# Mixer's second product: two images in every second slot, its followers a slot later, a quarter of the activations on ScalarE

## The reference, cut to what matters

```python
xh = _dht2d(x).reshape(B, H, W, nb, bs)
xn = jnp.roll(jnp.flip(xh, axis=(1, 2)), shift=(1, 1), axis=(1, 2))
...
o1k = relu(0.5 * (xh w1a + xn w1b) + b1[0])
o1n = relu(0.5 * (xn w1a + xh w1b) + b1[1])
...
o2k = 0.5 * (o1k w2a + o1n w2b) + b2[0]
o2n = 0.5 * (o1n w2a + o2k w2b) + b2[1]
y = (o2k + o2n).reshape(B, H, W, C)
y = jnp.sign(y) * jax.nn.relu(jnp.abs(y) - SPARSITY)
y = _dht2d(y) / (W * C)
return y + bias
```

## Time and profile before

| | us |
|---|---|
| median of 3 runs | 110.15 (109.63 to 111.55) |
| the profiled execution | 110.37 |
| its span in the trace | 108.6 |
| slots 8 and 9 (start of line 792's first matmul to start of slot 10) | 23.94 to 29.05 |
| slots 10 and 11 | 29.05 to 36.42 |
| slots 12 to 15 | 36.42 to 47.68 |
| slots 16 to 19 | 47.68 to 60.10 |
| slot 20 up to its first line 732 | 60.10 to 62.45 |

### The profile page before, as it was taken

One profiled execution on the slowest core, in us unless ns is written; L12 is line 12 of the kernel. 1 busy time (PEld: TensorE's weight loads), 2 busy tenths in 40 slices (PEclk: granted clock), 3 DMA queues, 4 the chain that ended last, 5 costly groups with the idle time before them and its releaser, 6 DMA issues.

```text
span 108.6 us, 2853 instructions
## 1 busy us (share of the span) xinstructions
PE 100.9 (93%) x1008; PEld 87.7 (81%) x1008; DVE 70.3 (65%) x282; ACT 63.6 (59%) x186; POOL 55.2 (51%) x107
## 2 busy tenths in 40 slices
PE   5799999999999999999889799998899999999990
PEld 4488898988898799988669598875899999999670
DVE  1117687786877787773534879797576956665761
ACT  5036985928643776646426595867566557667520
POOL 1108500000888598885004264669998997753300
PEclk9999999999999999999999999999999999999999
DMA  2898800000000000000000000000000010011122
GB/s 73 245 348 227 329 12 6 0 3 0 3 0 6 0 0 0 6 0 0 0 6 0 0 12 0 0 0 6 0 0 0 0 48 31 26 48 51 48 68 77
DMA packets 3182, 4.57 MB, mean 42 GB/s; under 512 B 480, under 2 KB 2400, under 8 KB 3168
## 3 DMA queue, kind: packets, MB, share of 16 engines
q1 hardware_dynamic: 2160, 2.61, 7.3%
q10 hardware_dynamic: 1008, 1.78, 5.0%
HBM read 3.34 MB, written 1.05 MB: 40 GB/s over the span
## 4 chain that ended last, share of the span: by engine, by line
PE 77%; DVE 5%; POOL 4%; ACT 4%; DMA 3%; issue 3%; POOLq 1%; SPq 0%; DVEq 0%
PE banks L732 10%; PE banks L634 8%; PE banks L726 8%; PE banks L706 7%; PE banks L673 6%; PE banks L663 5%; PE banks L829 4%; PE banks L690 4%; PE banks L847 4%; DMA xt_in<-in_x_t 3%; PE banks L792 3%; PE banks L646 3%; PE banks L616 3%; PE banks L872 2%; PE banks L808 2%
## 5 line engine op out<-in xcount | busy, mean ns | idle before, releaser
L533 POOL TENSOR_SCALAR hidden<-first,ident_columns 64x260 f32<-64x260 f32 x16 | 19.7, 1230 | 18.6 <-DVE first L1241 17.7
L982 ACT ACTIVATE probs<-negated,lowest 128x256 f32<-128x256 f32 x48 | 23.9, 499 | 6.9 <-DVE negated L1139 6.8
L481 POOL TENSOR_TENSOR probs<-probs,inverse 128x256 f32<-128x256 f32 x30 | 17.9, 614 | 16.0 <-DVE inverse L1153 15.6
L990 ACT ACTIVATE probs_t<-banks 128x512 f32<-128x512 f32 x22 | 13.1, 595 | 9.9 <-PE banks L706 9.8
L732 PE MATMUL banks<-probs_t,v 128*128 128x256 f32 x56 | 15.2, 395 | 0.0
L1153 DVE RECIPROCAL inverse<-total 128x1 f32<-128x1 f32 x48 | 7.6, 160 | 10.3 <-ACT probs L982 9.8
L706 PE MATMUL banks<-ident_columns,probs 128*128 128x128 f32 x88 | 13.3, 273 | 0.0
L1139 DVE TENSOR_SCALAR_CACHE_REDUCE negated<-banks 128x256 f32<-128x256 f32 x32 | 12.1, 416 | 0.6 <-issue 0.2
L706 PEld LDWEIGHTS banks<-ident_columns,probs 128*128 128x128 f32 x88 | 10.5, 141 | 0.8 <-POOL probs L481 0.2
L732 PEld LDWEIGHTS banks<-probs_t,v 128*128 128x128 f32 x56 | 9.8, 190 | 1.2 <-issue 0.2
L1145 DVE TENSOR_SCALAR_CACHE_REDUCE negated<-banks,v 128x256 f32<-128x256 f32 x16 | 7.1, 482 | 4.7 <-PE banks L673 4.6
(11 more groups left out here) (122 smaller groups left out, 208.6 us busy)
## 6 DMA issues: line engine op xcount, KB each, us to landing
out<-stream SPq DMA_DIRECT2D x7, 128.0 KB, 2.0
rows<-in_x_rows ACTq DMA_DIRECT2D x1, 768.0 KB, 6.2
xt_in<-in_x_t SPq DMA_DIRECT2D x1, 512.0 KB, 5.3
constants<-in_constants SPq DMA_DIRECT2D x1, 450.0 KB, 5.6
layer<-in_layer ACTq DMA_DIRECT2D x1, 256.5 KB, 3.6
xt_in<-in_x_t SPq DMA_DIRECT2D x2, 128.0 KB, 3.6
xt_in<-in_x_t SPq DMA_DIRECT2D x1, 256.0 KB, 4.4
rows<-in_x_rows ACTq DMA_DIRECT2D x1, 256.0 KB, 4.7
```

What stands on the lines that cost most here:

```text
L481: pool.tensor_tensor(probs[:, half(job), tile, :], probs[:, half(job), tile, :], inverse[:, at, tile:tile + 1].to_broadcast([TILE, TOKENS] ...
L533: pool.tensor_scalar(halves(hidden[HC:C, half(job), side]), strided(first[own, half(job)], SUMS, -SUMS, SUMS), column["b1n"][own], 0.0, AL ...
L982: nc.scalar.activation(probs[:, half(job), tile, :], negated[:, half(job), tile, :], ACT.Exp, bias=lowest[:, half(job), tile:tile + 1], sc ...
L990: nc.scalar.activation(flat(probs_t[:, half(job)]), probs_t_bank, ACT.Copy).then_inc(probs_t_ready, 1)
```

## The change

Four things are done together.

- `second_product` runs for two images in a row, in the slots in which the younger of them is two slots old and odd. Images 0 and 1 have it in slot 11, 2 and 3 in slot 13, 4 and 5 in slot 15, 6 and 7 at the start of slot 17. ACT's `shrink_top` and DVE's `shrink` follow in pairs. `hidden` has four buffers in place of two.
- All that follows (`backward_channels`, `turn`, `backward_tokens`, `move_g`, `move_turned`, `add_turned`) belongs to the image four slots back in place of three, and so ends in slot 19 in place of 18. `turn` is now directly behind `backward_channels`.
- Images 5, 6 and 7 (before: 6 and 7) have their results in bank 4, so their `turn` waits for `move_g`, and `backward_channels` of images 6 and 7 waits for `add_turned` of the image before. `g` always goes through bank 4.
- Of the four parts of the relu one moves from POOL to ACT: `activate_last`, one activation with a bias, at the very end of ACT's slot. POOL keeps one part, DVE its two.

```diff
+def shares_g_bank(job):
+    return job.image >= BATCH - 3
+def mixed_pair(job):
+    return mixes(job) and job.image % PAIR == PAIR - 1
...
-        hidden = sb("hidden", [C, 2, 2, FREQ])
+        hidden = sb("hidden", [C, 4, 2, FREQ])
...
-            return banks[:, 4 if job.image >= BATCH - PAIR else 6 + half(job), :]
+            return banks[:, 4 if shares_g_bank(job) else 6 + half(job), :]
...
             def activate_other(job):
...
-                for side in range(2):
-                    own = slice(side * HC, (side + 1) * HC)
-                    pool.tensor_scalar(
-                        halves(hidden[HC:C, half(job), side]),
...
+                pool.tensor_scalar(
+                    halves(hidden[HC:C, i % 4, 0]), strided(first[0:HC, half(job)], SUMS, -SUMS,
...
             def energies_of_pair(job):
-                    pe.wait_ge(layer_done[MIXER], BATCH - PAIR)
+                    pe.wait_ge(layer_done[MIXER], BATCH - 3)
...
             def backward_channels(job):
-                if i == BATCH - 1:
+                if i > BATCH - 3:
                     pe.wait_ge(layer_done[MIXER], i)
...
             def turn(job):
-                if i >= BATCH - PAIR:
+                if shares_g_bank(job):
                     pe.wait_ge(g_ready, i + 1)
...
             # TensorE, slot(now)
+                if mixed_pair(back2) and not mixes(this):
+                    second_product(back3)
+                    second_product(back2)
...
-                if mixes(back2) and by_age(now, 4, 3):
-                    second_product(back2)
                 if by_age(now, 4, 3):
                     mix_values(by_age(now, 4, 3))
-                if mixes(back3):
-                    backward_channels(back3)
-                if mixes(back2) and not by_age(now, 4, 3):
+                if mixes(back4):
+                    backward_channels(back4)
+                    if not shares_g_bank(back4):
+                        turn(back4)
+                if mixed_pair(back2) and mixes(this):
+                    second_product(back3)
                     second_product(back2)
                 if mixes(this):
                     first_product(this)
...
-                if mixes(back3):
-                    turn(back3)
-                    backward_tokens(back3)
+                if mixes(back4):
+                    if shares_g_bank(back4):
+                        turn(back4)
+                    backward_tokens(back4)
...
+            def activate_last(job):
+                i = job.image
+                act.wait_ge(first_ready, i + 1)
+                if i >= 4:
+                    act.wait_ge(y_psum, i - 3)
+                nc.scalar.activation(
+                    halves(hidden[HC:C, i % 4, 1]), strided(first[HC:C, half(job)], SUMS, -SUMS,
+                                                            SUMS),
+                    ACT.Relu, bias=column["b1n"][HC:C]).then_inc(last_act_ready, 1)
...
             # ScalarE, slot(now)
-                if mixes(back2):
+                if mixed_pair(back2):
+                    shrink_top(back3)
                     shrink_top(back2)
                 if mixes(this):
                     move_of_sums(this)
-                if mixes(back3):
-                    move_turned(back3)
+                if mixes(back4):
+                    move_turned(back4)
+                if mixes(this):
+                    activate_last(this)
```

More of the change, by code:

```diff
@@ L528, in activate_other @@
                 pool.wait_ge(first_ready, i + 1)
[L529 to L536 removed]
+                if i >= 4:
+                    pool.wait_ge(y_psum, i - 3)
+                pool.tensor_scalar(
+                    halves(hidden[HC:C, i % 4, 0]), strided(first[0:HC, half(job)], SUMS, -SUMS,
+                                                            SUMS),
+                    column["b1n"][0:HC], 0.0, ALU.add, ALU.max).then_inc(other_act_ready, 1)
             def normalize(job):
@@ L830, in second_product @@
                             halves(o), second[:, side],
-                            strided(hidden[:, half(job), side], at, step, TILE // 2),
+                            strided(hidden[:, i % 4, side], at, step, TILE // 2),
                             start=True, stop=True)
@@ L900, in slot @@
             def slot(now):
-                this, back1, back2, back3 = (job_at(now, k) for k in range(4))
+                this, back1, back2, back3, back4 = (job_at(now, k) for k in range(5))
                 mean_pair, variance_pair = (completed_pair(job_at(now, k)) for k in (5, 6))
+                if mixed_pair(back2) and not mixes(this):
+                    second_product(back3)
+                    second_product(back2)
                 if plain_pair(back2):
@@ L1008, in move_g @@
                 act.wait_ge(g_psum, job.image + 1)
-                nc.scalar.activation(flat(g[:, half(job)]), g_bank(job),
+                nc.scalar.activation(flat(g[:, half(job)]), g_bank,
                                      ACT.Copy).then_inc(g_ready, 1)
+            def activate_last(job):
+                i = job.image
+                act.wait_ge(first_ready, i + 1)
+                if i >= 4:
+                    act.wait_ge(y_psum, i - 3)
+                nc.scalar.activation(
+                    halves(hidden[HC:C, i % 4, 1]), strided(first[HC:C, half(job)], SUMS, -SUMS,
+                                                            SUMS),
+                    ACT.Relu, bias=column["b1n"][HC:C]).then_inc(last_act_ready, 1)
             def move_turned(job):
                 act.wait_ge(back_psum, job.image + 1)
+                if job.image >= 2:
+                    act.wait_ge(layer_done[MIXER], job.image - 1)
                 nc.scalar.activation(turned[:, half(job)], result_bank(job)[:, TOKENS:2 * TOKENS],
@@ L1017, in slot @@
             def slot(now):
-                this, back1, back2, back3 = (job_at(now, k) for k in range(4))
+                this, _, back2, back3, back4 = (job_at(now, k) for k in range(5))
                 if by_age(now, 4, 3):
@@ L1228, in shrink @@
                     dve.wait_ge(mixer_ready, 6)
+                if i >= 2:
+                    dve.wait_ge(g_psum, i - 1)
                 nc.vector.scalar_tensor_tensor(
@@ L1246, in activate @@
                 dve.wait_ge(first_ready, i + 1)
-                if i >= 2:
-                    dve.wait_ge(y_psum, i - 1)
+                if i >= 4:
+                    dve.wait_ge(y_psum, i - 3)
                 for side in range(2):
                     own = slice(side * HC, (side + 1) * HC)
-                    nc.vector.tensor_scalar(hidden[0:HC, half(job), side], first[own, half(job)],
+                    nc.vector.tensor_scalar(hidden[0:HC, i % 4, side], first[own, half(job)],
                                             column["b1k"][own], 0.0, ALU.add, ALU.max).then_inc(
@@ L1296, in slot @@
                     sum_means(completed_pair(mixed))
-                if mixes(back3):
-                    add_turned(back3)
+                if mixes(back4):
+                    add_turned(back4)
                 if plain_pair(back2):
```

27 lines of the change are left out of this document (13 added, 14 removed).

## The result

The changed kernel takes 114.91 us (median of 7 runs, 114.51 to 118.74) against 109.94 (7 runs of the kernel before). The ratio is 1.044 (95% interval 1.041 to 1.048): 4.9 us slower by the ratio, 5.0 by the medians. Some executions of most kernels here take 2 to 4 us longer and are left out of the ratios; the profiled one of the changed kernel is such (118.74 us), and as it lost its time ahead of slot 8, which began at 27.40 us and not at 23.94, it is read from slot 8 on. From there to the end it takes 116.9 - 27.40 = 89.5 us against 108.6 - 23.94 = 84.7: 4.8 us more.

What follows compares the result with a forecast made beforehand. The prediction took PE to bound the kernel: new PE stops of 8.1 us, less 2.9 of stops that go and 0.8 of switches, give 4.4 us more on the profiled 110.37, so 114.8 us; range 112.3 to 116.4.

Steps and rivals of the forecast that it cites:

- PE's stops are what counts in the mixer: Slots 12 to 15: PE busy 11.26 us of 11.26, so only its stops count; taking work from POOL alone gains nothing.
- ACT's wait for `first` ahead of `probs_t`: Slots 9 to 11: `activate_last` waits for DVE's `first` and delays `probs_t`; PE stops of 1.50, 1.21 and 1.21 us.
- The ring: Slots 10 and 11: round of waits from line 726 through `first`, `activate_last` and `probs_t` to the next 726, 3.55 us.
- `z` late in slots 12 and 14: `z` stands behind `activate_last` on ACT, so line 808 waits: PE stops of 0.82 and 0.36 us.
- Three round trips over `g`, and `y` behind `g` on ACT: Slots 16 to 19: PE waits for `g`, and once for image 7's `y`: stops 0.42, 0.64, 0.69, 0.64, 0.64 us.
- The stop in slot 20 goes: The 0.68 us wait for DVE's weights ahead of line 634 in slot 20 disappears.
- The delay passes to the end undiminished: Behind line 732 the order is untouched and everything awaited moved with it, so no delay is given back.
- The switches, 0.76 us: Pairing second products leaves four changes of matmul width instead of eight, saving 4 x 0.19 us; by the drain rule 0.43.
- The sum: Whole kernel: stops that come 8.1 us, stops that go 2.9, switches 0.8, together 4.4 us more.
- (a): Rival: `first` is always ready when ACT comes, so its wait costs nothing; 110.1 us, no change; chance 0.09.
- (b): Rival: pairing hides the round trips over `g` too and, with (a), only gains stay; 106.7 us; chance 0.03.
- (d): Rival: PE's clock halves in slots 9 to 12 through idleness; about 120 us; chance 0.02.

Runs made afterwards that it cites:

- experiment 1: The changed kernel with both upper parts of the relu made by POOL again, pairs, late slot and bank 4 kept: 111.30 us, ratio 1.014.
- experiment 10: On experiment 8's kernel, slots 8 to 10: transposes ahead of the first product, ACT's `probs_t` copy ahead of `of_sums`: 110.08 us, ratio 1.0005.
- Experiment 4: The changed kernel with `backward_channels` of images 5 to 7 earlier in slots 17 to 19, other PE work between it and `turn`: 113.41 us, ratio 1.033.
- experiments 1 to 3: experiment 1, experiment 2, and the kernel before with only a relu quarter moved from POOL to the end of ACT's slot: 113.32 us, ratio 1.030.
- experiment 8: The kernel before with `backward_channels` of image 7 moved ahead of layer 2's projections in slot 18: 109.02 us, ratio 0.993.
- experiment 2: The changed kernel with ACT's relu activation moved behind the next slot's copies of `probs_t`, `z` and `g`: 110.77 us, ratio 1.009.

## Why the prediction was right

The forecast was 114.8 us with a range of 112.3 to 116.4, and 114.91 was measured. Point by point:

- **PE's stops are what counts in the mixer; work off POOL is worth nothing there.** Right: POOL lost 4.5 us of load in slots 12 to 15 and the slots got longer; and taking the quarter back (experiment 1) made the kernel faster. It is right for this order only: in experiment 10 POOL is on the path.
- **ACT's wait for `first` ahead of `probs_t`.** Right in place and mechanism. Forecast stops of 1.50, 1.21 and 1.21 us, measured 31.85 - 30.23 = 1.62 (line 799 starts at 29.78 and takes 0.45), then 1.33 and 1.33. The ring is 3.66 us and not 3.55. The term that was mis-sized is the distance from `activate_last` to `probs_t`: 0.53 us for the 0.40 taken from the exponential. It lies above the upper bound of the prediction too (0.49), because the overlap is missing that each of the prediction's rows had.
- **`z` late in slots 12 and 14.** Forecast stops 0.82 and 0.36, measured 0.89 and 0.47, in the main from the same 0.13 us.
- **Three round trips over `g`, and `y` behind `g` on ACT.** Forecast 0.42, 0.64, 0.69, 0.64, 0.64; measured 0.42, 0.63, 0.64, 0.63, 0.64. Experiment 4 removes the three ahead of line 870, and shows what the prediction didn't have: that DVE's order is the next thing behind them.
- **The stop in slot 20 goes.** Right: line 641 has no idle ahead of it at 69.81, and line 739 follows at 70.83.
- **The delay passes to the end undiminished.** Right: 46.07 us against 46.15.
- **The switches, 0.76 us.** Too small. Two images took 2 x (0.59 + 0.42) = 2.02 us for lines 829 and 808 in the chain; a slot with a pair takes 1.02 + 0.42 for the same two lines, and the slot without one 0.23. The chain of the changed kernel in slot 13:

```profile
46.12 1.02 PE banks L837 x16
47.14 0.42 PE banks L815 x2
47.56 0.24 PE banks L817 x2
```

  That is 0.35 saved per pair, 1.4 in all if the four pairs save alike: 0.19 for the width, as forecast, and 0.16 since 16 passes take 1.02 and not 2 x 0.59. The drain at a change of tiling mode that the Trainium skill, TensorEngine Tiling (Array Packing), Key Properties, states agrees with the trace in kind: 0.10 us more on the way into line 837 (line 870 has 0.32 to the next start and not 0.22) and 0.10 on the way out (line 815 0.33 and not 0.22). The estimate of 0.43 us by the drain's length that the Trainium skill, TensorE: Matmul & The Clock Gate, Part 2, gives was the worse one.
- **The sum.** The forecast had 4.4 us more, and the traces differ by 4.8. Stops measured: 1.62 + 1.33 + 1.33 + 0.89 + 0.47 + 2.96 = 8.6 for the 8.1 forecast; the saving 1.4 for 0.8. The prediction left out that a group of matmuls behind a stop often takes longer: line 733 0.99 us to the next line's start where 0.95 is usual, line 815 0.33 for 0.22, line 870 0.28 for 0.22, line 697 nothing. Over the ten stops after that makes about 0.6 us, over those before about 0.1. So 8.6 - 2.9 - 1.4 + 0.5 = 4.8: errors of opposite sign, of which the saving's was the largest.
- **The number.** That 114.8 and 114.91 agree to 0.1 us is luck. The forecast started from the profiled execution, 110.37, which lies 0.4 above the median of the seven runs, 109.94; its increase was 0.4 to 0.6 too small, and the two cancel.
- **Rivals.** (a), ACT's wait costs nothing, falls with experiments 1 to 3: in slot 9 `first` ended 0.7 us later than (a) needed. (b), the round trips over `g` are hidden, falls with the three rows of 0.47. (d), the clock falls, didn't come: it stayed at 1.00 through slots 10 and 11, where PE is busy 5.77 of 8.11 us. The rule of the Trainium skill, TensorE: Matmul & The Clock Gate, Part 1, that an idle TensorE is gated to half speed did not come into play at this idleness.

What the change was worth apart from these two costs: with both removed it stands at 0.996, with DVE's order mended at 0.992, where one move in the old kernel stands as well (0.993). With slots 8 to 10 rearranged too, the kernel with pairs comes to 0.988. The comparison that counts is with the best kernel without pairs, experiment 8's 0.993, and there the intervals overlap: from slot 8 to layer 2's first `mix_values` the traces have 60.54 - 23.17 = 37.37 us and 62.97 - 25.44 = 37.53. So a gain of the pairs themselves is not shown; the same rearrangement cost the kernel without pairs its gain (1.0005).

## What to carry to other kernels

An instruction that is cheap and off the path still holds up all that stands behind it in its engine's list: before putting one at a list's end, find what it waits for and who waits for the next entry. In a software pipeline put it behind the copies that feed the bound engine. And when a stage moves, look at each producer and consumer that become neighbours on the bound engine: of a round trip to another engine the bound engine loses all that it has no work for (here 0.64 of 1.19 us), unless other work is put between.

## What the hardware showed beyond expectation

- Second products of two images in one go: 16 passes on 64 columns take 1.02 us, 8 take 0.59. The saving from grouping, 0.35 us a pair, was nearly twice the cost of the change of width alone, 0.19.
- An activation that reads and writes partitions 64 to 127 didn't overlap with its neighbours on ACT. The next one started 0.53 us after the start of one of 0.51, and 0.41 after one of 0.38; in experiment 2, where it had nothing to wait for, it started 0.41 after the start of a `g` of 0.38. Where `z` is followed by `g` in the changed kernel, it is 0.29 after one of 0.39.
- A group of matmuls behind a stop took 0 to 0.11 us longer than the same group without one (line 733 0.99 for 0.95, line 815 0.33 for 0.22).
